# First attention operands loaded within the last image's convolutions, and low relative parts formed by TensorE and ScalarE

## What is computed

```python
kqv = jnp.einsum('bhwc,co->bhwo', x, qkv_w) + qkv_b       # k, q, v: 64 channels each
logits = jnp.einsum('bnid,bnjd->bnij', qf, kf)            # 8 heads, 1024 x 1024
rel_w = rel_logits_1d(qh, key_rel_w, H, W, (0, 1, 2, 4, 3, 5))
rel_h = rel_logits_1d(qh_t, key_rel_h, W, H, (0, 1, 4, 2, 5, 3))
weights = jax.nn.softmax(logits + rel_w + rel_h, axis=-1)
attn = jnp.einsum('bnij,bnjd->bnid', weights, vf)
```

## Time and profile before

| | |
|---|---|
| median of 3 runs | 2158.36 us (2155.96 to 2159.87) |
| the profiled execution | 2156.28 us |
| its span | 2154.5 us, mean granted clock 0.96 |
| TensorE busy | 2032.2 us (94%) |
| VectorE, ScalarE, POOL busy | 1419.5 (66%), 1272.9 (59%), 255.2 us (12%) |
| DMA | 268.08 MB, 124 GB/s mean |

### The profile page before, as it was taken

One profiled execution on the slowest core, in us unless ns is written; L12 is line 12 of the kernel. 1 busy time (PEld: TensorE's weight loads), 2 busy tenths in 40 slices (PEclk: granted clock), 3 DMA queues, 4 the chain that ended last, 5 costly groups with the idle time before them and its releaser, 6 DMA issues. The chain is left out here.

```text
span 2154.5 us, 27575 instructions
## 1 busy us (share of the span) xinstructions
PE 2032.2 (94%) x10056; PEld 1389.9 (65%) x10056; DVE 1419.5 (66%) x2090; ACT 1272.9 (59%) x2189; POOL 255.2 (12%) x277
## 2 busy tenths in 40 slices
PE   5999999589999999999999998999999969999997
PEld 4788888455554445544444446777777748888886
DVE  6766775477777777777777655666666544656655
ACT  4344543137777777777777766666666645656654
POOL 2000000102222222221222300000000000000000
PEclk8999999559999999999999999999999989999999
DMA  3334454967687777776666522323331145443341
GB/s 117 93 106 163 162 203 164 178 210 123 112 117 111 109 108 115 121 110 115 106 115 107 151 94 82 112 94 113 105 107 63 40 154 201 160 156 137 137 152 53
DMA packets 144070, 268.08 MB, mean 124 GB/s; under 512 B 23489, under 2 KB 87745, under 8 KB 139969
## 3 DMA queue, kind: packets, MB, share of 16 engines
q1 hardware_dynamic: 136128, 241.12, 46.4%
q0 software_dynamic: 7680, 25.17, 3.7%
q10 hardware_dynamic: 128, 0.03, 0.0%
HBM read 156.37 MB, written 107.24 MB: 122 GB/s over the span
## 5 line engine op out<-in xcount | busy, mean ns | idle before, releaser
L789 DVE TENSOR_REDUCE a_nmax<-a_sm 128x1 f32<-128x1024 f32 x512 | 603.4, 1220 | 191.4 <-PE a_sm L809 191.4
L1081 ACT ACTIVATE p_shared<-a_st 128x512 f32<-128x512 f32 x1024 | 556.6, 596 | 240.3 <-PE a_st L1109 239.1
L1124 PE MATMUL a_pv<-p_shared,a_va 128*32 128x512 f32 x2048 | 272.5, 604 | 0.0
L1109 PE MATMUL a_st<-a_qf,a_kf 121*128 121x512 f32 x704 | 251.9, 437 | 3.5 <-PEq L1148 2.2
L1109 PEld LDWEIGHTS a_st<-a_qf,a_kf 121*128 121x128 f32 x704 | 118.8, 189 | 196.0 <-ACT p_shared L1081 184.9
L809 PE MATMUL a_sm<-a_kf,a_qf 120*128 120x512 f32 x704 | 219.3, 432 | 25.1 <-DMA a_kf<-kq_d 19.2
L2104 DVE SCALAR_TENSOR_TENSOR x_h_lo<-x_hid,x_wts,x_h_hi 128x512 fp32r<-128x512 f32 x128 | 96.0, 751 | 139.7 <-ACT x_h_hi L2065 139.6
L809 PEld LDWEIGHTS a_sm<-a_kf,a_qf 120*128 120x128 f32 x704 | 135.1, 202 | 75.2 <-issue 42.2
L2194 PE MATMUL x_h_ps<-x_v_hi,x_w 128*128 128x512 f32 x512 | 183.3, 399 | 0.0
L2208 PE MATMUL x_y_ps<-x_h_hi,x_w 128*128 128x512 f32 x512 | 180.7, 394 | 0.0
L2061 ACT ACTIVATE x_hid<-x_h_ps,x_bias 128x512 f32<-128x512 f32 x128 | 88.1, 688 | 139.7 <-PE x_h_ps L2194 139.7
(11 more groups left out here) (291 smaller groups left out, 3391.4 us busy)
## 6 DMA issues: line engine op xcount, KB each, us to landing
x_w<-w_d SPq DMA_DIRECT2D x31, 1024.0 KB, 8.6
rel_d<-p_shared SPq DMA_DIRECT2D x14, 2048.0 KB, 11.5
a_qf<-rel_d SPq DMA_DIRECT2D x22, 512.0 KB
a_qf<-rel_d SPq DMA_DIRECT2D x44, 256.0 KB
c_xtok<-in_x SPq DMA_DIRECT2D x8, 1024.0 KB, 5.9
va_d<-c_va SPq DMA_DIRECT2D x16, 512.0 KB, 5.3
a_va<-va_d SPq DMA_DIRECT2D x32, 256.0 KB, 23.5
a_w_st<-in_L_ffn_W POOLq DMA_DIRECT2D x32, 256.0 KB, 9.2
```

Source lines behind the costliest of these rows:

```text
L789: nc.vector.tensor_reduce(nmax[:, h, t:t + 1], sm[k % 2][:], axis=AX.X, op=ALU.max, negate=True).then_inc(sm_read, 1)
L1081: nc.scalar.activation(probs[:, t % 2, h, half * HALF:(half + 1) * HALF], st[half][:], ACT.Exp).then_inc(exp_done, 1)
L1109: nc.tensor.matmul(st[half][:], kf[j][0:ROW_M + 1, h, t * P:(t + 1) * P], qf[j][0:ROW_M + 1, h, 2 * t // TT, half * HALF:(half + 1) * HALF ...
L1124: m = nc.tensor.matmul(pv[32 * h:32 * h + 32, cols], va[j][:, t, h, :], probs[:, t % 2, h, cols], start=t == 0, stop=t == TT - 1, skip_gro ...
```

## The change

In the last image, unit `c0,2` is put ahead of the eight relative pieces 4. In the convolutions' block, POOL makes the one-hot mask once image 8's statistics are done. After `c0,2` of the last image, ScalarE and VectorE wait for the mask and for all stores of keys and queries, and write the one-hot rows of group 0's keys (two heads each). SP, after this image's stores of keys and queries, issues the load of group 0's queries, waits for the one-hot rows, and issues the keys; the store of relative pieces 4, of values and of results come behind. POOL doubles the queries of group 0 as they land. For this, buffers of the convolutions that are dead by then (input, normalized image, one slot of `v`, some weights) are placed where group 0's queries and keys will be; self-attention buffers are placed there later.

In the attention's first block, the logits begin at once. The low part of a relative piece is no longer made by VectorE: ScalarE copies the high part, TensorE adds minus the high part to the piece in its accumulator by one matmul of 512 columns with a negated identity (`"rest"`), and ScalarE copies what remains. The new order is one step of logits, then eight rounds (piece, rest of the piece before, logits), eight steps of logits, eight such rounds with the second table, and the other steps.

```diff
-            UNITS[:5] + rel(4, 0, 8) + UNITS[5:] + rel(5, 0, 8)]
+            UNITS[:6] + rel(4, 0, 8) + UNITS[6:] + rel(5, 0, 8)]
...
                     if ahead:
                         load(b + 2)
+                    if b == B - 1:
+                        sp.wait_ge(unit_done, done(b, "v", 2))
+                        sp.wait_ge(v_ready, 4 * B)
+                        load_queries(sp, kq_d, rel_d, 0, group.queries, group.twice_loaded, group.loaded)
+                        sp.wait_ge(group.built, 2)
+                        load_keys(sp, kq_d, 0, group.keys, group.loaded)
                     if FIRST <= b:
                         store_relative(b, RELS_OF[b][0])
...
+                pool.wait_ge(gvar_ready, B)
+                nc.gpsimd.memset(group.ones_hot[:], 0.0)
...
+                pool.wait_ge(group.twice_loaded, 16 * group.TWICE)
+                for h in range(HG):
+                    nc.gpsimd.tensor_copy(group.queries[0:ROW_H[0], h, 1, :], group.queries[0:ROW_H[0], h, 0, :]).then_inc(group.doubled, 1)
...
                         elif what == "c0" and t == 2:
                             if prefetch:
                                 spread(b + 1)
+                            else:
+                                act.wait_ge(group.made, 1)
+                                act.wait_ge(kq_stored, KQ_DMAS * 16 * (B + 1))
+                                act.wait_ge(unit_done, done(b, what, t))
+                                for h in range(HG // 2, HG):
+                                    last = nc.scalar.activation(group.keys_of(h), group.both_halves, ACT.Copy)
+                                last.then_inc(group.built, 1)
...
+                            if what == "c0" and t == 2 and not prefetch:
+                                dve.wait_ge(group.made, 1)
+                                dve.wait_ge(kq_stored, KQ_DMAS * 16 * (B + 1))
+                                dve.wait_ge(q_ready, B)
+                                for h in range(HG // 2):
+                                    last = nc.vector.tensor_copy(group.keys_of(h), group.both_halves)
+                                last.then_inc(group.built, 1)
...
-        order = rels[:RU] + passes[:13]
-        for i in range(RU // 2):
-            order += rels[RU + 2 * i:RU + 2 * i + 2] + passes[13 + i:14 + i]
-        order += passes[13 + RU // 2:]
+        SECOND = 16
+        order = passes[:1]
+        for k, p in enumerate(passes[1:]):
+            for i, at in ((0, 0), (1, SECOND)):
+                if at <= k < at + RU:
+                    order.append(("rel", i, k - at))
+                if at < k <= at + RU:
+                    order.append(("rest", i, k - at - 1))
+            order.append(p)
...
-                load_queries(sp, 0, 0)
-                sp.wait_ge(built[0], 2)
-                load_keys(sp, 0, 0)
                 store_last()
-                load_queries(sp, 1, 1)
+                load_queries(sp, kq_d, rel_d, 1, qf[1], doubled_loaded[1], loaded[1])
                 load_v(sp, 0, 0)
                 sp.wait_ge(built[1], 1)
-                load_keys(sp, 1, 1)
+                load_keys(sp, kq_d, 1, kf[1], loaded[1])
                 store_relative(0)
                 load_v(sp, 1, 1)
                 store_relative(1)
...
+                        act.wait_ge(rel_read, piece(what, i, n))
...
-                        nc.vector.tensor_tensor(rel_target(hl_lo[r], wh, n), rel_ps[n % BANKS][:],
-                                                rel_target(bits(hl_hi[r]), wh, n), ALU.subtract).then_inc(rel_lo, 1)
...
+                    if what == "rest":
+                        pe.wait_ge(made, 2)
+                        pe.wait_ge(rel_read, piece("rel", i, n))
+                        r = TURNS[i]
+                        nc.tensor.matmul(rel_ps[n % BANKS][:], minus[:], rel_target(hl_hi[r], RELS[r][0], n),
+                                         start=False, stop=True, skip_group_check=True).then_inc(rel_done, 1)
+                        continue
```

230 lines of the change are left out of this document (122 added, 108 removed).

## The result

The changed kernel takes 2162.48 us (median of 20 runs, 2156.14 to 2167.44) against 2158.28 us for the kernel before (20 runs): a ratio of 1.0018, 95% interval 1.0010 to 1.0027. It is slower by 0.18%; the forecast was 2146.3. The profiled execution is the shortest of the changed kernel's, 2156.14 us with a span of 2154.4.

The account below looks back on a forecast made before the run. TensorE was taken as the bound nearly everywhere, except at the seam between convolutions and attention. 2156.28 - 19.1 (block) + 7.0 (last image) = 2144.2, plus 2.1 to the median: 2146.3 us; range 2125 to 2153.

Parts of the forecast that it names:

- The round of 2.99 us: Attention's first block: piece 1.71, rest 0.43 and logits 0.85 us make one round, paced by TensorE.
- the block of 76.5 us: Attention's first block takes 76.5 us instead of 95.6, a gain of 19.1 us.
- rival (a): Clock comes up in the first block's rounds or never falls at the seam: 2125.3 us, or 2136; chance 0.24.
- The wait for the first keys: Start of the attention's first block: TensorE's 19.2 us of waiting goes, as the loads move into the last image.
- rival (d): First logits still wait, for keys or doubling; only together with rival (c), within its chance of 0.05.
- the account of the gain: First block: 19.2 us of waiting plus 5.4 of hidden VectorE pacing minus 6.8 for sixteen rests; gain 19.1 us.
- the stall of the last image: Near 346 us TensorE stands 2.7 us behind the one-hot copies and the clock falls; loss 7.0 us.
- Cost 0, up to 5: Last image: pieces 4's store lands at 377 us, before the last eight pieces begin at 379.
- part 3: What the last image pays for the change: loss 7.0 us, between 2.6 and 8.5.
- rival (c): SP's queue: slow load rows delay the last image's store to 424 us; 41 us lost, 2187 us; chance 0.05.
- whatever the seam gives or costs moves the end by as much: Seam between convolutions and attention: TensorE is full for the whole main attention afterwards, so every gain or loss reaches the end.
- Rival (b): Gain eaten by a longer last-image stall and two waits for stores, 5 us each: 2153 to 2158 us; chance 0.10.

Follow-up runs that it names:

- second profile: The changed kernel run once more, unchanged: 2160.47 us, ratio 1.0013 to the kernel before.
- late keys: Changed kernel with c0,2 back behind the eight pieces, table 1 stored first, and group 0's keys issued after the values' store: 2146.3 us, ratio 0.9937.
- halfway: Late keys with two of four slow query transfers before pieces 4's store, two and the keys after: 2138.23 us with VectorE's low parts, 2140.52 with TensorE's.

## Why the prediction was wrong

**Right: the block.** The round of 2.99 us, measured 2.99; the block of 76.5 us, measured 76.4 (393.77 to 470.1, where the last maximum ends); the clock 0.50 in the rounds, so rival (a) stayed out. It came up only for some 3.5 us where the first rounds had ended (0.99 from 419 to 420, 1.00 to 422), never within one. The rule of the Trainium skill ("TensorE: Matmul & The Clock Gate", "What's actually happening") that activity releases the throttle, taken plainly, did not agree with these gapless rounds either. The wait for the first keys went, and rival (d) did not come. Two things in the account of the gain were off and made no difference to the block: it charges sixteen rests (6.8 us) where its own sum has fourteen in the rounds (6.0), which is most of the 1.3 us it left as rounding; and VectorE's subtractions did cost something, 1.1 us at the ends of the rounds.

**Right in mechanism, wrong in size: the stall of the last image.** The stop near 347 was 0.92 us, not 2.7: the stores of keys and queries had landed by 343.4, not 345.0, and VectorE's part was out of the way. The clock fell all the same, until 357.6 instead of about 360. c1,1 was read 5.1 us later than before (358.88 against 353.82), against the 7.0 of the sum. Putting c0,2 back took the stall and the fall away.

**Failed: "Cost 0, up to 5" for the store of pieces 4.** The prediction took 19.3 us from the earlier trace rows, which is a median from issue to landing, where what counts is the later of two transfers. ScalarE went on after 26.6 us. The wait was 4.31 us on ScalarE and 3.98 on TensorE, and the clock fell again: the last four pieces took 1.71 us each instead of 0.9. Of the 12.3 us that the last image lost, 5.1 were there at c1,1 and the other 7.2 came here, where the sum had 0; since the first stall was 1.9 cheaper than forecast, part 3 as a whole was 5.3 too cheap (12.3 less 7.0). The rows for it were there: 0.94 busy at 127 GB/s. They were used in rival (c) alone, and there doubled, though the view counts the bytes of a transfer once: in the trace of before the store of 2 x 2048 KB passes at 374 GB/s in 11 us (350 to 361), that is 4.1 MB and not 8.4. At 127 GB/s that rival's landing would have been 33 us after issue, beside the 26.6 measured: not a mishap of 0.05, but nearly the case that came, with a price of some 8 us (391 less 383) and not 41.

**Failed: "whatever the seam gives or costs moves the end by as much".** This is the step that took the rest of the gain. TensorE is full behind the block only as long as each group's load lands in time, and the second block's transfers hang on the tables' stores, not on the block's start. The prediction counted the tables' stores among the queues and asked only what the block's own end waits for. It never asked what waits for their landing in the block behind. They were issued at 454.87 and 458.27, so the fill for group 2 gained 1.3 us where its reader gained 6.8, and TensorE waited for the rest. The swap of the two stores showed it, and the second rounds 8 steps earlier showed it again.

**The sum of it.** With 7.0 replaced by 12.3 and 7.1 added for the wait, 2156.28 - 19.1 + 12.3 + 7.1 gives 2156.6; the profiled execution took 2156.14. With the last image alone set right, 6.8 us of gain would have been left. The median lies 6.3 us higher, where the prediction had added 2.1 for it. The second profile, with its wait of 8.76 us, shows that this wait varies; that it explains all of the 6.3 is not shown. Rival (b), the gain eaten, had 2153 to 2158. The profiled execution lies in it and the median, 2162.48, does not; the nearness is luck, for (b) knew one of the two costs, the last eight pieces that wait for their store, and the other, 7 to 10 us in the second block, no rival had. (The lower end of the forecast's own range, 2140, should by its terms be 2141.4; nothing hangs on it.)

**The version that came out of it.** Loads split around the store with two of the four slow transfers on either side, c0,2 in its old place, table 1 stored first, low parts from VectorE: 2138.23 us, 0.9904 [0.9887, 0.9920] of the kernel before. Of these 20 us the early loads alone gave 8.2 (2149.98 against 2158.13 in its series); the rest is the order on SP's queue that fits them, and the new order of the block without the rest matmul.

## What to carry to other kernels

When a stage is made shorter, follow every transfer that the next stage needs back to what lets it start; where that is a store near the stage's end, the gain can stop there: here one store moved was worth 12 to 15 us, when the stage's own gain was 6.8. Price a transfer that is put in front of a store by the bytes and the rate of its slowest part, and take the last landing, not the median. A step that frees an engine which nothing waits for (VectorE's subtraction, hidden at 2.56 us a round) and adds work to the one that all wait for loses that work, wherever that engine sets the pace: fourteen of sixteen matmuls, 6.0 us, of which 4.2 were left at the end of the block.

## What the runs showed of the hardware

- Where the transfers into 16 partitions (4 KB rows) were under way, the DMA engines' share was 0.91 to 1.21 at 61 to 100 GB/s (changed kernel and late keys); with those into 32 partitions it was 189 to 227. The store from 128 partitions moved at 408 to 412 alone (before, 352 to 360), and one row with it reached 422. In front of the store, the four slow ones took some 12 us for 1 MB (349 to 361), two of them some 6 us for half of it (349 to 355, halfway). Why is not shown.
- The same store of 2 x 2048 KB held its source for 26.6 to 30.2 us behind these transfers (changed kernel, late keys 27.8, c0,2 back 30.2); without them in front its two transfers landed after a median of 9.3 us.
- TensorE's granted clock fell to 0.50 after a stop of only 0.92 us in the midst of relative pieces, and stayed there until 357.6; a gapless row of 128-column pieces from 347.5 to 354.3 did not bring it back.
- The granted clock in the thin stretch from 1280 to 1320 differs between executions with the same code (0.56 against 1.00), and goes with up to 6.4 us more from the self-attention to the experts (478.7 against 472.3).
